# Gathered expert rows in a GNN and mixture-of-experts kernel: turned by a transposing DMA instead of by TensorE

## What is computed

```python
proj = jnp.einsum('bsd,ed->bse', x, Wp)
gate_scores = jnp.einsum('bsd,ed->bse', _l2norm(proj), _l2norm(sim_matrix)) / temperature
top_v, top_i = jax.lax.top_k(gate_scores, 2)
gate_probs = jax.nn.softmax(top_v, axis=-1)
comb = jnp.sum(jax.nn.one_hot(top_i, E) * gate_probs[..., None], axis=-2)
h = jax.nn.gelu(jnp.einsum('bsd,edf->ebsf', x, W1) + b1[:, None, None, :], approximate=False)
eo = jnp.einsum('ebsf,efd->ebsd', h, W2) + b2[:, None, None, :]
out = jnp.einsum('ebsd,bse->bsd', eo, comb)
```

## Time and profile before

| what | value |
|---|---|
| median of three runs | 2280.35 us (2278.39 to 2281.62) |
| span of the profiled execution | 2278.0 us |
| PE busy | 1924.5 us (84%) |
| DVE busy | 1502.1 us (66%) |
| ACT busy | 1126.8 us (49%) |
| POOL busy | 873.5 us (38%) |
| HBM read and written | 419.17 MB and 81.17 MB |

### The profile page before, as it was taken

How to read it: one execution, slowest core, us unless ns; L and a number is a source line. 1 busy time by engine, 2 the same in 40 slices (tenths; PEclk the granted TensorE clock), 3 DMA queues, 4 the chain that set the end, 5 groups by cost and what they waited for, 6 DMA issues and landing times. The chain is left out here.

```text
span 2278.0 us, 53767 instructions
## 1 busy us (share of the span) xinstructions
PE 1924.5 (84%) x14846; PEld 1304.6 (57%) x14847; DVE 1502.1 (66%) x4361; ACT 1126.8 (49%) x2449; POOL 873.5 (38%) x1357
## 2 busy tenths in 40 slices
PE   5888886755679999989999588873999999999997
PEld 3555554554368888878888455542454454455553
DVE  6776765888767777777777799967543443443333
ACT  3233432111158788878878566645543443443332
POOL 1002002998046666666666111102232332332322
PEclk9998998755799999999999799996999999999999
DMA  6333344341069999999999677746546646545542
GB/s 254 100 110 116 114 154 142 127 181 60 0 226 362 355 349 361 354 349 356 350 355 353 208 220 222 220 144 266 205 158 254 225 150 248 220 162 167 180 159 72
DMA packets 136017, 490.18 MB, mean 215 GB/s; under 512 B 17250, under 2 KB 17458, under 8 KB 133760
## 3 DMA queue, kind: packets, MB, share of 16 engines
q0 software_dynamic: 99168, 347.42, 44.3%
q1 hardware_dynamic: 36768, 141.71, 17.1%
HBM read 419.17 MB, written 81.17 MB: 220 GB/s over the span
## 5 line engine op out<-in xcount | busy, mean ns | idle before, releaser
L1045 PE MATMUL main_ps<-rows,O 128*128 128x256 f16 x4992 | 573.8, 273 | 48.7 <-DVE acc L981 29.0
L1028 ACT ACTIVATE O<-O,pk 128x128 f16<-128x128 f16 x1664 | 499.2, 387 | 121.8 <-DVE O L998 120.7
L1045 PEld LDWEIGHTS main_ps<-rows,O 128*128 128x128 f16 x4992 | 464.1, 98 | 115.5 <-DVE acc L981 34.1
L967 POOL DMA_INDIRECT rows<-projected,idx x416 | 394.9, 949 | 195.7 <-issue 81.1
L1002 DVE TENSOR_SCALAR O<-O,pk 128x128 f16<-128x128 f16 x1664 | 320.2, 267 | 14.7
L1779 PE MATMUL pj_ps<-gram,xsT 128*125 128x512 f16 x1200 | 288.9, 401 | 48.4 <-ACT xsT L394 48.2
L1730 PE MATMUL x_h<-w_p,gram 128*128 x1344 | 305.7, 385 | 18.1 <-ACT gram L1683 8.8
L1745 PE MATMUL x_o<-w_p,gram 128*128 x1344 | 308.1, 379 | 1.4 <-ACT gram L1699 1.4
L1779 PEld LDWEIGHTS pj_ps<-gram,xsT 128*125 128x125 f16 x1200 | 169.2, 145 | 156.3 <-ACT xsT L394 56.9
L1730 PEld LDWEIGHTS x_h<-w_p,gram 128*128 128x128 f16 x1344 | 131.3, 99 | 169.7 <-issue 29.0
L1745 PEld LDWEIGHTS x_o<-w_p,gram 128*128 128x128 f16 x1344 | 129.1, 98 | 147.3 <-issue 1.8
(11 more groups left out here) (346 smaller groups left out, 2586.8 us busy)
## 6 DMA issues: line engine op xcount, KB each, us to landing
w_f<-in_L_ffn_W_dram SPq DMA_DIRECT2D x14, 2048.0 KB, 13.9
b_t<-in_L_ffn_b_dram SPq DMA_DIRECT2D x56, 512.0 KB, 3.7
projected_f<-xp_f POOLq DMA_DIRECT2D x25, 500.0 KB, 3.7
projected<-xp POOLq DMA_DIRECT2D x25, 500.0 KB, 4.7
out_dram<-n_x POOLq DMA_DIRECT2D x25, 500.0 KB, 8.0
x_after_gnn_normed<-PK POOLq DMA_DIRECT2D x25, 500.0 KB, 4.3
xt<-in_x_dram SPq DMA_DIRECT2D x24, 512.0 KB, 3.3
n_own<-projected_f SPq DMA_DIRECT2D x24, 512.0 KB, 6.5
```

Source lines behind the costliest of these rows:

```text
L967: pool.indirect_dma_start(out=rows[:, 4 * p + k, :, :].rearrange("k n d -> k (n d)"), out_offset=None, in_=xp_d[:, :], in_offset=bass.Indi ...
L1028: ins = act.activation(O[:, k, 1 + HEADS + h, :], O[:, k, 0, :], ACT.Copy, scale=pk[:, p, k, w:w + 1])
L1045: pe.matmul(main_ps[:, h * C:(h + 1) * C], O[:, k, 1 + HEADS * a + h, :], rows[:, 4 * p + k, b, h * C:(h + 1) * C], start=first and h % 2 ...
```

## The change

The rows of a tile are turned by a DMA that transposes on the way from `xg` to `xgT`, SBUF to SBUF, and that ACT issues at the place where it copied. PE no longer has `turn`, and the tile x_tr is gone. ACT waits for the gather and for the product that last read the buffer before it issues. `first` waits for the DMA's semaphore, now one for each buffer, and the gather waits for that one too.

```diff
-        s_xi, s_tr = sem("xp_xi"), sem("xp_tr")
+        s_xi = sem("xp_xi")
+        s_xT = [sem(f"xp_xT{p}") for p in range(2)]
...
-        def gather(pool, i, p):
+        def gather(pool, i, p, turned=0):
             if not early(i, 2):
-                pool.wait_ge(s_tr, i - 1)
+                pool.wait_ge(s_xT[p], 16 * ((i - 2) // 2 + 1) if isinstance(i, int) else 16 * turned)
                 pool.wait_ge(s_xi, i - 1)
...
-                    def take_x(i, p):
-                        act.wait_ge(s_tr, i + 1)
+                    def turn(i, p, g):
+
                         if not early(i, 2):
-                            act.wait_ge(s_h, i - 1)
-                        act.activation(xgT[:, p, :, :, :], tr_ps[:, :, :, :], ACT.Copy).then_inc(s_xT, 1)
+                            wait_apart(act, s_met, s_h, i - 1)
+                        wait_apart(act, s_met, s_g[p], g)
+                        act.dma_start_transpose(xgT[:, p, :, :, :].rearrange("p n k c -> p (n k) c"),
+                                                xg[:, p, :, :].rearrange("t n d -> t (n d)")).then_inc(s_xT[p], 16)
...
                         if not (isinstance(i, int) and i == XTILES - 1):
-                            take_x(i + 1, 1 - p)
+                            turn(i + 1, 1 - p, 16 * (j + 1 + p))
...
-                    take_x(0, 0)
+                    turn(0, 0, 16)
...
-                    def turn(i, p, g):
-                        pe.wait_ge(s_g[p], g)
-                        if not early(i, 1):
-                            pe.wait_ge(s_xT, i)
-                        turn_parts(pe, tr_ps, xg[:, p, :, :], ident16).then_inc(s_tr, 1)
...
-                        pe.wait_ge(s_xT, i + 1)
+                        pe.wait_ge(s_xT[p], 16 * (j + 1))
...
-                        q_ago = first(i, p)
+                        q_ago = first(i, j, p)
                         if not early(i, 1):
                             second(i - 1, 1 - p, q_ago, 0)
-                        if not (isinstance(i, int) and i == XTILES - 1):
-                            turn(i + 1, 1 - p, 16 * (j + 1 + p))
-                        if not early(i, 1):
                             second(i - 1, 1 - p, q_ago, 1)
                         turn_h(i)
-                    turn(0, 0, 16)
```

More of the change, by code:

```diff
@@ L1549, in program @@
             b2_t = sbuf(c, "b2_t", [P, 2, D])
-            tr_ps = c.enter_context(nc.psum_tensor("x_tr", [P, 2, KD, P], F16))
             ht_ps = c.enter_context(nc.psum_tensor("x_ht", [P, 2, KF, P], F16))
@@ L1558, in program @@
             s_st = [sem(f"xp_st{p}") for p in range(2)]
-            s_xT, s_h, s_hb, s_gel = sem("xp_xT"), sem("xp_h"), sem("xp_hb"), sem("xp_gelu")
+            s_h, s_hb, s_gel = sem("xp_h"), sem("xp_hb"), sem("xp_gelu")
             s_hi, s_lo, s_ht, s_hT, s_o, s_eo = sem("xp_hi"), sem("xp_lo"), sem("xp_ht"), sem("xp_hT"), sem("xp_o"), sem("xp_eo")
@@ L1633, in body @@
                         if not (isinstance(i, int) and i >= XTILES - 2):
-                            gather(pool, i + 2, p)
+                            gather(pool, i + 2, p, j + 1)
                         if not early(i, 1):
@@ L1712, in _, with first @@
                 def _(pe):
-                    def turn(i, p, g):
-                        pe.wait_ge(s_g[p], g)
-                        if not early(i, 1):
-                            pe.wait_ge(s_xT, i)
-                        turn_parts(pe, tr_ps, xg[:, p, :, :], ident16).then_inc(s_tr, 1)
-                    def first(i, p):
+                    def first(i, j, p):
                         e, q, q_ago, _, _, _ = tile_word(pe, i)
                         pe.wait_ge(s_wlo, WPIECES * (e + 1))
-                        pe.wait_ge(s_xT, i + 1)
+                        pe.wait_ge(s_xT[p], 16 * (j + 1))
                         if not early(i, 1):
```

## The result

The changed kernel takes 2468.23 us (median of 4 runs, 2455.77 to 2480.00) beside 2280.74 us for the kernel before on the same chip: a ratio of 1.0825, 95% interval 1.0797 to 1.0854. It is 187 us slower.

A forecast was written before the change was run, and what follows sets the result against it. PE was taken as the bound, with the turn's landing closing a chain: 43 x 12.6, 8 x 18.2 and splits 8 make 695.4 against 611.0, so +84; opening +20; 2280.35 + 104 = 2385 us, range 2265 to 2640.

The forecast's parts named there:

- The bound and the loop: Expert stage: PE is the bound; after the change x_h, h_b, Gelu, h_s, DMA, next x_h form a closed chain.
- Break-even: Plain tile: L, the turn's time from issue to landing, must be 4.0 us to match the old 11.70 us period.
- A plain tile: Expert-stage tile away from weight loads: period 7.7 us plus a landing of 4.9, so 12.6 us; 43 such tiles.
- Idle for 1.8 I charge nothing: PE's clock in plain tiles: 1.8 us idle before x_h keeps full clock, so no time is added.
- its line at 2.5: PE's clock: idle of 2.5 us or more before x_h halves it and makes x_h 1.7 us longer.
- the clock falls too: Rival, chance 0.25: landing of 5.6 us or more, every x_h at half clock; 2537 us at 6.5, about 2650 at 8.5.
- The eight longest tiles: Tiles beside a weight load, two for each of four loads: landing 8.8 us, period 18.2 us with the clock loss.
- the one on splits: Ten tiles where DVE splits weights: h_b 2.6 us late, 0.8 remaining on the closed chain, 8 us in all.
- Opening: Tiles 0 to 3: 5 us more for each, 20 us in all.
- As fast as a plain load: Rival, chance 0.13: the turn lands after 3.7 us, 5.6 beside a weight load; total 2295 us.
- hidden: Rival, chance 0.10: the turn lands within 3.2 us in every tile, PE stays the bound; total about 2252 us.
- Piece by piece: Rival, chance 0.10: each small piece costs a mean packet, so the turn lands after 17.9 us; total 3113 us.

The follow-up runs named there:

- experiment 1: The changed kernel with the turn of tile i+1 issued at the head of ACT's work for tile i, ahead of the wait for Gelu's input: 2315.68 us, ratio 1.0162.
- the last kernel with paced loads: The changed kernel, turn still behind h_s, each 4 MB weight load in four 1 MB parts over four tiles, each issued after that tile's turn landed: 2421.26 us.

## Why the prediction was right in sign and short in size

**The bound and the loop: right.** PE's own work without the transposes is 10.80 us a tile, x_h waits for the DMA into gram, and moving the issue off the loop took 152 us away. Of the 51 x_h one waited last for something else by the profile, DVE's split in tile 23. Break-even was put at L = 4.0. No turn landed before 4.2 us, and the best periods, 11.83 us in tiles 53 and 54 with no gather left beside the turn, did not beat 11.70.

**A plain tile: 12.6 predicted, 13.5 measured.** This term was mis-sized, in three pieces. The 42 periods up to 15 us have a mean of 13.49, over the 13.3 that the prediction had set as the sign of too short an L. From x_h to the issue is 7.15 after a full-clock x_h, not 7.7, since the issue begins while h_s still runs (2165.65 and 2165.84 in the timeline of ACT): -0.5. From the issue to the next x_h is 5.66 on average, not 4.9: +0.8. And 16 of the 42 had an x_h that began at half clock, 1.76 longer: +0.7. "Idle for 1.8 I charge nothing" took the mean idle time for that of every tile; in fact the landings swing. Timeline of PE, three tiles on end:

```profile
2273.76 7.04 PE L1726 MATMUL x_h<-w_p,gram 128*128 x24 [3.23 <-issue]
...
2287.17 5.35 PE L1726 MATMUL x_h<-w_p,gram 128*128 x24 [0.74 <-DMA gram<-gram]
...
2301.59 6.98 PE L1726 MATMUL x_h<-w_p,gram 128*128 x24 [3.45 <-issue]
```

A long landing makes PE idle for 3.2 us, and its clock falls; the slower x_h puts the next issue 1.7 us later, when less is in flight, and that turn takes 4.6 from issue to x_h instead of 7; PE idles for 0.74 only, the clock is back, and so on. What is in flight shows in the DMA views of the first and the second of these turns, from issue to landing (2282.6 to 2286.9 and 2294.3 to 2301.3 us):

```profile
q10 hardware_dynamic: 2080, 0.52, 65.1%
...
gram<-gram ACTq DMA_TRANSPOSE x1, 4.2
```

```profile
q0 software_dynamic: 264, 0.95, 45.9%
...
gram<-gram ACTq DMA_TRANSPOSE x1, 6.9
```

The first turn has the engines to itself; the second shares them with 264 packets of POOL's queue (the gather, which lands 5.6 us after its issue). Of the 52 x_h from tile 4 on, 21 began at half clock; in the first 2.2 us of tile 36's the granted clock was 0.51. The idle times on which the clock was judged held only at the ends: all of 2.79 us or more were followed by the low clock and all of 2.11 or less by the full one, but 2.12 (tile 36) and 2.74 were followed by the low one, 2.35, 2.56 and 2.78 by the full one. By the prediction's own sign, x_h of 5.34 us after idle times over 2.5 and of 7 after shorter ones, its line at 2.5 was wrong. The 3.3 us of the earlier trace rows were not one idle time either but two, of 2.62 and 0.70 us, with 0.62 us of work between them. The larger miss is the spread of L, which was left out. So the rival "the clock falls too" came true in two tiles of five. Over the 43 tiles of the sum (these 42 and tile 36, with 16.2) this is 582.7 us, against 541.8 + 8: 33 of the missing 83 us.

**The eight longest tiles: 18.2 predicted, 22.6 measured.** That there are eight is luck. The prediction gave each of four loads two tiles; one tile a load had its turn beside it (9, 16, 23 and 30), and the other four long ones (8, 15, 22 and 29) are tiles that split weights. Beside a load the price was too low: L = 8.8, read off a gather beside a load, against landings of 7.9, 18.1, 17.4 and 19.7, and a mean period of 25.2. A gather moves its 512 KB in packets of some 3 KB (its queue's mean from 1600 to 2470 us, 74.72 MB in 23616 packets) and a turn in packets of some 250 bytes; the row was nearest in size and place, not in packet size. In the other four the step that failed is the one on splits, a late h_b that costs 0.8 us: their turn takes 8.9 to 14.7 us to land with no load beside it (in tile 8 only the last 2 us), for which the prediction had no term, and their mean period is 19.9, against 12.6 + 0.8 = 13.4. The eight take 180.5 us, against 145.6: 35 us.

**Opening: 20 predicted, 29.5 measured.** The price beside a load again; the turn of 25.6 us sits there.

**The remaining 5 us**: 2.5 in the span outside the 51 periods and the opening (184.2 - 181.7), and 3 between the growth of the profiled span (184.2) and that of the medians (187.5).

**Covers that were named.** ACT's hT copy behind the issue was said to be covered by the following x_h. It was: x_h came later still, even where the issue held ACT for 8.45 us. But the prediction had no term for an issue that holds its engine; experiment 1 shows that it becomes one as soon as the issue stands ahead of Gelu.

**Rivals.** "As fast as a plain load" and "hidden" fell on the landing: 5.5 in the median and 4.2 alone, where they needed 3.7 and 3.2. "Piece by piece" fell too: no plain turn takes 17.9. The Trainium skill, VectorE: DVE Perf Modes, section The three transpose paths, from whose figure an estimate of 20.9 us for 16 blocks one after the other was worked out, does not carry over: 16 blocks land after 4.2 us where nothing is beside them. Its preference for TensorE (section Rules for kernel authors) agrees with the outcome of every complete version here.

## What to carry to other kernels

Before work is moved from an engine to a DMA, ask on which loop its landing will lie, and put the issue at the earliest point at which its inputs are there: here two lines of placing were worth 152 us, and the transposes saved at most 50. Price a transfer of small pieces by its landing in company, beside the transfers that will cross it, and not by a plain transfer of as many bytes. And charge idle time by its spread, not its mean, since the clock punishes the long ones.

## What the runs showed that I had not expected

- The transposing DMA and a weight load passed packets one for one (563 and 570 in 6 us), and a turn of 512 KB took up to 25.6 us instead of 4.2. Smaller load pieces and another issuing queue did not remove this. Nor does it take a load: in five long periods of the change, and in the long turns of the last kernel with paced loads, none or nearly none was in flight, and a gather, a put and a b2 load that met a turn took 9.5 to 12.2 us with no load at all. What sets that price is open. Not tried: turning two tiles ahead with a third pair of buffers, and leaving the tiles beside loads to TensorE.
- Issuing a transposing DMA held its engine: 1.33 us at least, 3.23 in the median, 14.53 beside a load, against 1.02 for a 4 MB load's two issues by SP in the timeline above.
- With half the blocks the median hold fell to 1.25 us and the landing from 5.5 to 4.8 us in the median, from 4.2 to 3.0 at the shortest.
